# A recommendation tower on one core: first-chunk ids spread by matmuls, tables looked up as upper halves and bytes

## The reference

```python
e = jnp.stack([tbl_0[ids[:, 0]], ..., tbl_38[ids[:, 38]]], axis=1)     # 512 x 39 x 16
x0 = xk = e
for W in (W0, W1):                                                     # 39 x Hk x 128 each
    xk = jnp.einsum('bid,bjd,ijh->bhd', x0, xk, W.reshape(39, Hk, 128))
    outs.append(xk)
z = jnp.sum(jnp.concatenate(outs, axis=1), axis=-1)                    # 512 x 256
h = jnp.maximum(jnp.concatenate([z, dense_ctx], axis=1) @ W_top1 + b_top1, 0.0)
h = jnp.maximum(h @ W_top2 + b_top2, 0.0)
y = h @ W_top3
```

## Time and profile before

| | |
|---|---|
| median of 3 runs | 284.72 us (283.92 to 285.29) |
| the profiled execution: its time | 284.26 us |
| its span on the core | 282.5 us |
| mean granted TensorE clock, share of full | 0.952 |
| busy: TensorE, VectorE, ScalarE, GpSimd | 228.4, 163.8, 153.4, 136.8 us |
| DMA bytes | 12.58 MB |

### The profile page before, as it was taken

One profiled execution on the slowest core, in us unless ns is written; L12 is line 12 of the kernel. 1 busy time (PEld: TensorE's weight loads), 2 busy tenths in 40 slices (PEclk: granted clock), 3 DMA queues, 4 the chain that ended last, 5 costly groups with the idle time before them and its releaser, 6 DMA issues.

```text
span 282.5 us, 4480 instructions
## 1 busy us (share of the span) xinstructions
PE 228.4 (81%) x1548; PEld 190.5 (67%) x1548; DVE 163.8 (58%) x309; ACT 153.4 (54%) x298; POOL 136.8 (48%) x135
## 2 busy tenths in 40 slices
PE   0000349798988999984999999999999999999897
PEld 0000348455767777974977878999687799978696
DVE  6556660398875887535454786674566856542301
ACT  1133133599776897525384786654667857531301
POOL 4787777777777777777777777200000000000000
PEclk9999958669999999996899999999999999999999
DMA  4434640992210111111011012010101010000000
GB/s 78 112 121 123 169 128 9 251 284 33 28 29 10 26 23 21 29 19 19 6 17 22 9 26 31 7 24 3 23 2 17 8 25 9 15 15 12 2 0 0
DMA packets 29862, 12.58 MB, mean 45 GB/s; under 512 B 21438, under 2 KB 27672, under 8 KB 29840
## 3 DMA queue, kind: packets, MB, share of 16 engines
q1 hardware_dynamic: 25648, 11.22, 15.9%
q0 software_dynamic: 4192, 1.08, 4.6%
HBM read 9.66 MB, written 0.00 MB: 34 GB/s over the span
## 4 chain that ended last, share of the span: by engine, by line
PE 46%; POOL 34%; issue 13%; ACT 4%; DMA 2%; ACTq 0%
POOL emb L263 34%; PE turn_bank L340 10%; PE x_bank L305 5%; PE turn_bank L351 4%; PE x_bank L308 4%; PE x_bank L307 4%; PE pair_bank L288 4%; PE misc_bank L277 2%; PE turn_bank L374 2%; PE g_bank L328 2%; PE x_turn_bank L316 2%; PE g_bank L329 2%; PE g_bank L332 2%; ACT x1h L669 1%; ACT prod_hi L656 1%
## 5 line engine op out<-in xcount | busy, mean ns | idle before, releaser
L263 POOL DMA_INDIRECT emb<-tbl,ids_sb x131 | 136.6, 1043 | 42.1 <-issue 39.6
L651 ACT ACTIVATE prod<-pair_bank 128x512 f32<-128x512 f32 (+1 forms) x112 | 66.6, 598 | 46.9 <-PE pair_bank L288 46.9
L305 PE MATMUL x_bank<-prod_hi,pair_w_hi 128*128 128x512 f32 (+1 forms) x112 | 64.8, 579 | 4.5 <-ACT x1h L669 4.5
L531 DVE TENSOR_TENSOR prod_lo<-prod,prod_hi 128x512 fp32r<-128x512 f32 x96 | 62.1, 687 | 2.9
L288 PE MATMUL pair_bank<-x,sel 117*128 117x512 bf16 (+1 forms) x112 | 45.0, 407 | 7.8 <-ACT prod L651 6.2
L340 PE MATMUL turn_bank<-g_sb,w_sb 128*128 128x128 f32 x312 | 42.0, 277 | 0.6 <-ACT g_sb L684 0.6
L340 PEld LDWEIGHTS turn_bank<-g_sb,w_sb 128*128 128x128 f32 x312 | 40.2, 194 | 2.1 <-ACT g_sb L684 0.9
L656 ACT ACTIVATE prod_hi<-prod 128x512 fp32r<-128x512 f32 x64 | 40.3, 630 | 0.0
L308 PE MATMUL x_bank<-prod_hi,pair_w_lo 128*128 128x512 f32 x96 | 38.5, 401 | 0.0
L307 PE MATMUL x_bank<-prod_lo,pair_w_hi 128*128 128x512 f32 x96 | 38.3, 399 | 0.0
L521 DVE CAST prod_hi<-prod 128x512 fp32r<-128x512 f32 x48 | 21.5, 447 | 28.7 <-ACT prod L651 28.2
(11 more groups left out here) (92 smaller groups left out, 278.6 us busy)
## 6 DMA issues: line engine op xcount, KB each, us to landing
xblk<-xs SPq DMA_DIRECT2D x128, 20.0 KB
emb<-tbl,ids_sb POOLq DMA_INDIRECT x131, 2.5
tab<-small SPq DMA_DIRECT2D x2, 625.0 KB
wt<-w_top SPq DMA_DIRECT2D x2, 512.0 KB
small_ids_i<-small_ids SPq DMA_DIRECT2D x2, 500.0 KB
small_ids_i<-small_ids SPq DMA_DIRECT2D x1, 562.5 KB
tab<-small SPq DMA_DIRECT2D x1, 562.5 KB
wa<-pair_w_a SPq DMA_DIRECT2D x1, 448.0 KB, 14.8
```

Source lines behind the costliest of these rows:

```text
L263: pool.indirect_dma_start(out=emb[:, at:at + D], out_offset=None, in_=tables[f], in_offset=bass.IndirectOffsetOnAxis(ap=ids_sb[:, c * M + ...
L305: mm = pe.matmul(x1_bank[:, :], pair_w_hi[p, t, :], prod_hi[p, k % 2, t, :], start=(t == 0), stop=(t == FULL))
L531: dve.tensor_tensor(prod_lo[:, k % 2, t, :] if t < FULL else prod_hi[rows, k % 2, t, :], prod[rows, (NT * k + t) % RING, :], prod_hi[rows, ...
L651: act.activation(prod[0:ROWS[t], n % RING, :], pair_bank[n % 2][0:ROWS[t], :], ACT.Square).then_inc(sq_done, 1)
```

## The change

The ids of the small fields are now loaded once, transposed, as [25, 512] int32. ScalarE converts them to f16, and 25 matmuls with one column of an identity, broadcast over 125 columns, spread each field's 128 ids over 125 partitions in PSUM, from where ScalarE copies them (`keep_ids`). Each set of tables is loaded in two DMAs, of 112 and of 13 partitions. The tables are no longer split by subtraction: ScalarE copies the upper 16 bits of each word as bf16, and the two lower bytes as two bf16 numbers (`keep_table`). After the lookup, ScalarE copies the sums to `looked`, and VectorE joins them to float32 words in `emb` (`words`: low = byte1 x 256 + byte0, then upper OR low). These words then go through the same split as gathered rows, which for chunk 0 is done in two pieces: fields 0 to 15, and fields 16 to 38. The zeroing of `xblk` is cut in two, its second half later, and the orders of ScalarE's, VectorE's and TensorE's set-up work change. The gathers of GpSimd and the main loop stay, but for the counts that some waits wait for.

```diff
+        look_bank = [turn_bank, x1_bank, g_bank[1]]
+        id_bank = look_bank + [misc_bank, pair_bank[0], pair_bank[1], g_bank[0]]
...
             sp.dma_start(ids_sb[:, :], ids).then_inc(ids_in, 16)
+            sp.dma_start(ids_i[:, :], small_ids).then_inc(ids_t_in, 16)
+            sp.dma_start(eye_f[:, :], ident_f[0:NS, 0:NS]).then_inc(eye_in, 16)
             sp.dma_start(row_id[:, :, :], row_ids).then_inc(row_id_in, 16)
             for n, (f0, w, rows) in enumerate(SETS):
-                of_set = slice(f0 * CH, (f0 + w) * CH)
-                sp.dma_start(small_ids_i[:, of_set], small_ids[:, of_set].to_broadcast([SP, w * CH])).then_inc(small_ids_in[n], 16)
-                sp.dma_start(tab[n][:, :, :, :], small_tables[n].rearrange("f (p r) d -> p f (r d)", p=SP)).then_inc(tab_in[n], 16)
+                by_p = small_tables[n].rearrange("f (p r) d -> p f (r d)", p=SP)
+                for at in (slice(0, 112), slice(112, SP)):
+                    sp.dma_start(tab[n][at, :, :, :], by_p[at]).then_inc(tab_in[n], 16)
...
+            pe.wait_ge(ids_t_ok, 2)
+            for f in range(NS):
+                mm = pe.matmul(id_bank[f // 4][0:SP, f % 4 * CH:(f % 4 + 1) * CH],
+                               eye_h[:, f:f + 1].to_broadcast([NS, SP]), ids_h[:, 0:CH], start=True, stop=True)
+                if f % 4 == 3 or f == NS - 1:
+                    mm.then_inc(id_spread, 1)
...
-            def table_rest(n):
-            def table_lo(n):
...
+            def words(n):
+                f0, w, _ = SETS[n]
+                dve.wait_ge(looked_ok, n + 1)
+                low = low_word[:, f0 * D:(f0 + w) * D]
+                dve.scalar_tensor_tensor(low.rearrange("b (f d) -> b f d", d=D), looked[:, f0:f0 + w, 2, :], 256.0,
+                                         looked[:, f0:f0 + w, 1, :], ALU.mult, ALU.add).then_inc(low_ok, 1)
+                dve.wait_ge(low_ok, n + 1)
+                dve.tensor_tensor(emb[:, f0 * D:(f0 + w) * D].bitcast(I32).rearrange("b (f d) -> b f d", d=D),
+                                  looked[:, f0:f0 + w, 0, :].bitcast(I32), low.rearrange("b (f d) -> b f d", d=D),
+                                  ALU.bitwise_or).then_inc(words_done, 1)
...
             for n in range(len(SETS)):
                 one_hot(n)
-                table_rest(n)
-                table_lo(n)
-            split_rest(0, NS)
-            split_lo(0, NS)
...
+            zero_xblk(1)
+            words(0)
+            words(1)
+            split_rest(0, 0, SETS[2][0])
+            split_lo(0, 0, SETS[2][0])
...
+            words(2)
+            split_rest(0, SETS[2][0])
+            split_lo(0, SETS[2][0])
+            keep_turned(0, turn_bank)
...
+            def keep_ids(n):
+                for bank in range(id_banks(n - 1) if n else 0, id_banks(n)):
+                    act.wait_ge(id_spread, bank + 1)
+                    cols = slice(bank * 4 * CH, min((bank + 1) * 4, NS) * CH)
+                    last = act.activation(small_ids_h[:, cols], id_bank[bank][0:SP, 0:cols.stop - cols.start], ACT.Copy)
+                last.then_inc(small_ids_ok, 1)
+
+            def keep_table(n):
+                act.wait_ge(tab_in[n], 32)
+                f, r = SETS[n][1:]
+                act.activation(tab_parts[n][:, :, :, 0, :].rearrange("p f r d -> p (f r) d"),
+                               upper(tab[n][:, :, :, :].rearrange("p f r d -> p (f r d)")).rearrange("p (n d) -> p n d", d=D),
+                               ACT.Copy).then_inc(tab_hi, 1)
+                act.activation(tab_parts[n][:, :, :, 1:3, :].rearrange("p f r q d -> p (f r) q d"),
+                               low_bytes(tab[n][:, :, :, :]), ACT.Copy).then_inc(tab_low, 1)
...
+            act.wait_ge(eye_in, 16)
+            act.activation(eye_h[:, :], eye_f[:, :], ACT.Copy).then_inc(ids_t_ok, 1)
+            act.wait_ge(ids_t_in, 16)
+            act.activation(ids_h[:, :], ids_i[:, :], ACT.Copy).then_inc(ids_t_ok, 1)
+            keep_ids(0)
+            keep_ids(1)
+            keep_table(0)
+            keep_ids(2)
+            keep_table(1)
             keep_looked_up(0)
+            keep_table(2)
             keep_looked_up(1)
             act.wait_ge(pair_w_done, 1)
             act.activation(pair_w_hi[:, :, :], pair_w[:, :, :], ACT.Copy, scale=0.5).then_inc(pair_w_split, 1)
+            split_first(0, 0, SETS[2][0])
+            split_second(0, 0, SETS[2][0])
+            keep_looked_up(2)
+            split_first(0, SETS[2][0])
+            split_second(0, SETS[2][0])
+            keep_turned(0)
```

More of the change, by code:

```diff
@@ L102, in build_tower @@
             touch = sb_early("touch", [128, NT, M])
-            small_ids_i = sb_early("small_ids_i", [SP, NS * CH], I32)
+            ids_i = sb_early("ids_i", [NS, B], I32)
+            ids_h = sb_early("ids_h", [NS, B], F16)
+            eye_f = sb_early("eye_f", [NS, NS])
+            eye_h = sb_early("eye_h", [NS, NS], F16)
             small_ids_h = sb_early("small_ids_h", [SP, NS * CH], F16)
+            looked = sb_early("looked", [128, NS, 3, D])
+            low_word = sb_early("low_word", [128, NS * D], I32)
             row_id = sb_early("row_id", [SP, len(SETS), 10])
@@ L137, in build_tower @@
         row_id_in = sem("row_id_in")
-        small_ids_in = [sem(f"small_ids_in{n}") for n in range(len(SETS))]
+        eye_in = sem("eye_in")
+        ids_t_in = sem("ids_t_in")
+        ids_t_ok = sem("ids_t_ok")
+        id_spread = sem("id_spread")
         tab_in = [sem(f"tab_in{n}") for n in range(len(SETS))]
@@ L199, in upper, with low_bytes, pieces, id_banks @@
             return ap.bitcast(BF16).rearrange("p (n two) -> p n two", two=2)[:, :, 1]
-        def flat(ap):
-            return ap.rearrange("p f r d -> p (f r d)")
+        def low_bytes(ap):
+            return ap.rearrange("p f r d -> p (f r d)").bitcast(U8).rearrange(
+                "p (n d four) -> p n four d", d=D, four=4)[:, :, 0:2, :]
+        def pieces(c):
+            return c + 2
+        def id_banks(n):
+            return -(-(SETS[n][0] + SETS[n][1]) // 4)
         def gathers(c):
@@ L429, in _ @@
                     mm.then_inc(touched, 1)
-                pe.wait_ge(onehot_done, n + 1)
                 pe.wait_ge(tab_hi, n + 1)
[L432 to L435, removed]
+                pe.wait_ge(tab_low, n + 1)
+                pe.wait_ge(small_ids_ok, n + 1)
+                for r in range(rows):
+                    pe.wait_ge(onehot_done, sum(at[2] for at in SETS[:n]) + r + 1)
+                    for f in range(w):
                         mm = pe.matmul(look_bank[n][:, f * 3 * D:(f + 1) * 3 * D], onehot[n][:, r, f, :],
-                                       tab_parts[n][:, f, r, :, :], start=(r == 0), stop=(r == rows - 1))
+                                       tab_parts[n][:, f, r, :, :], start=(r == 0 and f == 0),
+                                       stop=(r == rows - 1 and f == w - 1))
                 mm.then_inc(looked_up, 1)
@@ L634, in keep_turned, with split_first, split_second @@
                                ACT.Copy).then_inc(x3_b, 1)
[L636 to L645 removed]
+            def split_first(c, f0=0, f1=M):
+                if c == 0:
+                    act.wait_ge(words_done, len(SETS) - (f1 < M))
+                if f1 == M:
+                    act.wait_ge(gathered[c], gathers(c))
+                wait(act, turned, 2 * c)
+                act.activation(parts[:, 0, f0:f1, :].rearrange("b i d -> b (i d)"),
+                               upper(emb[:, c * M * D + f0 * D:c * M * D + f1 * D]), ACT.Copy).then_inc(split_first_done, 1)
+            def split_second(c, f0=0, f1=M):
+                act.wait_ge(split_left, pieces(c) - (f1 < M))
+                wait(act, turned, 2 * c)
+                act.activation(parts[:, 1, f0:f1, :].rearrange("b i d -> b (i d)"),
+                               upper(rest[:, f0 * D:f1 * D]), ACT.Copy).then_inc(split_mid, 1)
             def square(k, t):
```

98 lines of the change are left out of this document (34 added, 64 removed).

## The result

The changed kernel is slower: 289.77 us median of 4 runs (288.52 to 290.14) against 284.89 us of the kernel before, measured beside it (4 runs, 283.92 to 285.29). The ratio of the two is 1.0172, 95% interval 1.0139 to 1.0205. The forecast was 282.7 us, with a range of 280.0 to 285.0: wrong in the sign, and outside the range. The profiled execution of the changed kernel took 289.46 us, its span 287.7.

What follows compares the result with a forecast made beforehand. GpSimd's gathers up to chunk 2's landing were taken to bound the kernel. Gathers -2.4 + 0.4 = -2.0 us, so profiled 284.26 - 2.0 = 282.3; the runs' median stands 0.46 higher: 282.7 us, range 280.0 to 285.0.

Steps and rivals of the forecast that it cites:

- What limits the time: Whole kernel: GpSimd's gathers up to chunk 2's landing at 129.65 us, then 152.8 us; an earlier loop start gains nothing.
- Start of the loop: Set-up on ScalarE, TensorE and loads: main loop starts at 33 to 40 us, taken as 36, instead of 54.
- The slack to 61: Wait for chunk 1's gathers: a loop start costs time only if it comes after 61 us.
- The 28 one-hot compares stay as they are: VectorE's set-up: the compares are unchanged; no cost to the gathers was put on them.
- The memset costs the gathers no more in its new place: Moved second half of the xblk zeroing on VectorE, 2.2 us; a gather inside the old memset lost only 0.14.
- No gather of 2 us: Sign to look for in the new trace: no gather lasts 2 us.
- Gone are L503 and L508, and what the new instructions cost: VectorE's set-up: removed subtractions give gathers back 2.4 us; new two-input instructions cost 0.4 (bounds 0 and 0.7); net -2.0.
- rival C: Gathers lose elsewhere the 2.0 us they save, to new instructions and the redealt loop: no change, 284.7 us; chance 0.17.
- Chance in the loop: Main loop: shifting VectorE's instructions against the gathers deals their losses again, allowed +-1 us.
- Rival D: Main loop: VectorE's instructions meet gathers at the full rate of chance, chunk 2 lands 4.5 us later: 287.2 us; chance 0.08.
- The clock: TensorE restarts chunk 1 at 1.2 GHz, costing at most 2.7 to 3.6 us inside the 7.23 us wait: none at the end.
- rival B: TensorE's clock stays up at chunk 2: 2.2 us more gained, 280.5 us; chance 0.32.

Runs made afterwards that it cites:

- gaps_c: Changed kernel with the two xblk zeroings put between the three sets of one-hot compares: 287.35 us against 285.05 for the kernel before, ratio 1.0081.
- spaced_d: Changed kernel with both zeroings early and compare sets 2 and 3 each waiting for the lookups of the set before: 284.0 us, ratio 0.9958 to the kernel before.
- psum_ids_b: Changed kernel with both zeroings early, compares reading f32 ids from PSUM in 64 instructions, keep_ids gone: 279.81 us beside 286.2 for the kernel before, ratio 0.9804.
- before_28: Kernel before the change, with its 28 one-hot compares run together and the table subtractions behind them: 423.6 us against 419.0 for the kernel before.
- early_zero: Changed kernel with both xblk zeroings ahead of the unbroken compares: 416.5 us against 417.5 for the kernel before.
- early_zero_b: Changed kernel with both xblk zeroings ahead of the unbroken compares, a repeat: 408.5 us against 418.9 for the kernel before.

## Why the prediction was wrong

**What limits the time: right.** The time follows chunk 2's landing, and the early start of the loop is worth nothing. From ScalarE's start on chunk 2 to the end of the span it is 152.8 us before, 152.4 changed, 152.5 in gaps_c and in spaced_d, and 152.1 in psum_ids_b, while the start itself lies between 125.55 and 135.31.

**Start of the loop: too early a figure, without consequence.** 42.88 us, not 36, and outside 33 to 40. ScalarE had to wait 8.33 us, until 36.51, for chunk 0's own gathers: the held gather made them late. The prediction had counted only the lookup path. In spaced_d, without a held gather, the loop starts at 34.32. The slack to 61 covered all of it, and the wait for chunk 1 was 17.14 us, as forecast ("about 15 us or more").

**"The 28 one-hot compares stay as they are": the step that failed.** Their number and form stay; their place doesn't. The same part of the prediction lists that the ids' broadcasts and L503 and L508 go, which were what kept the three groups apart, and doesn't ask how VectorE's queue looks without them. The gather at 9.92 lost 7.88 - 1.28 = 6.6 us against its neighbour at 8.33.

The Trainium skill, "SBUF — State Buffer", section "SBUF: two separate sides", says that an operation of VectorE in a two-port mode and a GpSimd operation exclude each other for a whole instruction, and the prediction named it but priced instructions with two inputs alone. The traces agree that these compares exclude a gather. The trace before the change had shown it too: the gather at 21.71 and six others that began beside compares took up to 1.41 us, 2.4 us over 0.94 in all, as much as L503 and L508 cost. Compares that read PSUM leave the gathers at 0.94 to 0.95 us, those with f32 ids at 1.01 to 1.16. The traces go beyond the rule in its size: by one instruction at a time a gather would lose at most the 0.41 us of a compare, and one was held through some 19 of them (7.88 us), in before_28 through some 22 (9.07 us).

**"The memset costs the gathers no more in its new place": failed too.** The gather beside it took 3.27 us, some 2.3 us more than 0.94. The 0.14 us of the row at 2.89 were taken for the price of any zeroing. In its new place the zeroing has L539, an instruction with two inputs in SBUF, ready behind it, and the gather ended at 26.82, 0.82 us behind L539's end. "No gather of 2 us" fell with both.

**Gone are L503 and L508, and what the new instructions cost: about the right size in the changed kernel, not in spaced_d.** Gathers 15 to 53 lost 2.35 us instead of 4.64: 2.3 us less, and the new instructions with two inputs cost the gathers of the set-up some 0.3 us, where 0.4 was forecast (the gather held at the zeroing aside). But in spaced_d the change without its held gathers comes to -1.05 us by the medians, and its 92nd gather starts no earlier than before (127.64 for 127.21), which is the forecast's rival C, nothing gained. Its new instructions cost 0.3 us too; the rest of the gain is lost beside old ones that met other gathers: 1.1 us more beside the pair weights and 1.5 us more in the loop (0.35 up to the 53rd gather, 1.16 behind it).

**Chance in the loop: inside the allowance in the changed kernel.** Gathers 54 to 92 lost 3.69 instead of 3.43 us. Rival D, which forecast 287.2 from these instructions, had the right sign by the wrong mechanism: it needed 4.5 us here, and 0.26 came. In the three other kernels that ran beside 285 us these gathers lost 4.47 to 4.61, so 1.04 to 1.18 us more than before, a little over the 1 us allowed.

**The clock.** The granted clock in one-microsecond windows of the changed kernel (busy PE, PEld, DVE, ACT, POOL, then PEclk, DMA share, GB/s):

```profile
133.00:134.00 1.00, 0.00 (x0) 0.00 (x0) 0.00 (x0) 0.00 (x0) 0.83 (x1) 1.00 0.23 29
136.00:137.00 1.00, 0.43 (x2) 0.34 (x3) 0.11 (x1) 1.00 (x4) 0.93 (x1) 0.57 0.12 20
139.00:140.00 1.00, 1.00 (x7) 1.00 (x7) 1.00 (x3) 0.29 (x1) 0.70 (x2) 0.72 0.04 3
```

It fell to 1.2 GHz all the same, before the first work at 136.57, and was back to 2.4 GHz within the window at 139: some 3 us of work at 1.2 GHz, instead of the 5.4 before. (The prediction read the earlier trace rows a little off: a mean of 0.76 in the window from 129 puts the fall at 129.5, 3.7 us behind the last matmul, and 0.83 in the one from 136 the return at 136.3.) The stretch behind it is 0.4 us shorter than before, but that this is the clock's doing isn't shown: in spaced_d the clock was low from 129.3 to 136.2, almost as before, and the stretch is 0.3 us shorter too. In psum_ids_b the clock stayed at 2.4 GHz from 119 to 277, and the stretch is 0.7 us shorter, where rival B reckoned with 2.2 (TensorE didn't stand before chunk 2 there, so the two cases differ in more than the clock).

**The sum.** Terms of the prediction: -2.4 + 0.4 = -2.0 us. Measured at the start of the 92nd gather: +7.7 in chunk 0's gathers (6.2 more beside compares, 2.3 at the second zeroing, 0.6 beside pair weights and a split, less the 1.45 of L503 and L508), -2.3 behind them, +0.3 in the loop, 5.7 in all. From ScalarE's start on chunk 2 to the end it is 0.4 less, and the spans differ by 287.7 - 282.5 = 5.2, as the profiled times do (289.46 - 284.26).

**What stays open.** Why an unbroken row holds a gather in six executions and none in the seventh; whether f32 ids free the gathers by their type or by the slower rate; and whether the instruction ready behind a zeroing is what holds a gather, which the traces suggest and no run tests. What the unbroken row costs in end time follows from the landing, as shown, and from no kernel in which it alone is undone and which ran beside 285 us.

## What to carry to other kernels

When an engine issues transfers in a steady pace and sets the time, look at what the change does to the order and the pauses of every other engine that can exclude it, and not only at which instructions come and go: a wait that disappears can close a gap that others used. A longer instruction that leaves the partner free can be the better one: the slowest of the three forms of compare gave the fastest kernel of those whose end times can be compared. Work without a deadline, such as a zeroing, belongs where a trace has shown it harmless; its price at one place is no price for another, because what stands ready behind it comes with it.

## What the runs showed of the hardware that was not expected

- A gather was held through an unbroken row of f16 compares for 6.03 to 9.47 us, far beyond one compare's 0.41 us, and ended 0.12 us behind the row's last one each time. Beside instructions with two inputs in SBUF a held gather ended 0.82 us behind the instruction's end (at 19.49, behind L635's end at 18.68 in the changed kernel).
- Whether the row holds a gather can't be told from the starts: with the same times to 0.01 us a gather took 1.28 us in early_zero and 8.68 in early_zero_b.
- A zeroing of 4.33 us at 14.63 let one gather pass in 0.95 us and held the next for 4.97, until 0.82 us behind the subtraction that followed it. Between the two starts that subtraction had become ready.
